# Feature sums of two layer norms folded on the vector engine, so that each takes one matmul with ones

## The chip, the cores and the metric

The kernel runs on one core of one Trainium2 chip. The metric is the device time of one execution in microseconds; it is measured several times, and the median is taken.

## What is computed

A small vision tower over 64 images. Each image becomes 37 tokens (36 patches and a class token) of 256 features. Four blocks follow, each added to the tokens after a layer norm: a selective scan, dense experts (8 routed ones, weighted by a router, and a shared one of four pieces), attention (16 heads of 16 features, causal, over the 37 tokens of an image), and a routed expert layer. The norm ahead of each block is what matters here:

```
def _layernorm(x, axis=-1, eps=1e-05):
    m = jnp.mean(x, axis=axis, keepdims=True)
    v = jnp.var(x, axis=axis, keepdims=True)
    return (x - m) / jnp.sqrt(v + eps)
...
h = h + _L0_ffn_ref(_layernorm(h, axis=-1), ...)
h = h + _L1_attn_ref(_layernorm(h, axis=-1), ...)
h = h + _L1_ffn_ref(_layernorm(h, axis=-1), ...)
```

These norms are computed in 32-bit floating point.

## The kernel before, in words

Features lie on the 128 partitions, in two halves (HALVES = 2), and tokens along the columns. The 2,368 tokens are worked on in 8 chunks of 296 columns (CH), 8 images each. The residual stream is `hF`, 128 x 2 x 2368; the normed one is `xn`, of the same form.

A sum over features is a sum over partitions and over the two halves. TensorE makes it: a 128 x 128 matrix of ones (scaled to give a mean) times the data, once for each half, both added up in one PSUM bank. One norm of a chunk goes through five helpers:

- `pe_mean` (L391): two matmuls over the halves of h, 296 columns each (L395).
- `dve_center` (L426): VectorE subtracts the mean, 592 columns at once, into xn.
- `act_square` (L410): ScalarE squares xn into `sq`.
- `pe_var` (L399): two matmuls over the halves of the squares (L403).
- `act_rstd` (L417, L420) and `dve_scale` (L433): logarithm and exponential on ScalarE for the reciprocal root, then VectorE multiplies.

Each engine has its own list of instructions, written out by hand, and the lists meet only through semaphores that count up. The norm of a chunk is woven into the work of the next one, for the two norms that matter here as follows.

**Dense experts** (570 to 756 us of the span; norm "attn"). `pe_moe`, `act_moe` and `dve_moe` (L557 to L658) go through the chunks; a chunk has 12 pieces (8 experts and 4 of the shared expert; 8 in the first two chunks). For a piece TensorE makes the up product (two matmuls, L526), ScalarE its ReLU (L609), VectorE the gate and the square (L642, L648; only L648 for the shared pieces), and TensorE two down products two steps later (L585). Chunk c - 1's mean comes on TensorE ahead of step 5 of chunk c, its variance ahead of step 8; VectorE centres it after piece 5, ScalarE squares it after piece 6; the reciprocal root and the scaling come behind the last piece, then VectorE adds the result to hF (L655). SP loads the next gates when that add is done (L663).

**Attention** (756 to 965 us; norm "moe1"). `pe_step`, `act_step` and `dve_step` go through the chunks in four steps each, p = 0 to 3, two images a step. TensorE: turn the probabilities (L1322), the values' products (L1285), the outputs' products (L1339), the score products two steps ahead (L1273), and turn the outputs (L1364). VectorE: mask and row maximum and subtraction of the next step's scores (`soften`, L1985, L1990, L1992), reciprocal and scaling of the outputs (L2015, L2023), and the spreading of values (L2004, L2007). ScalarE: copy of the turned probabilities (L1684), the exponential (L1668), copies of the turned outputs (L1697, L1698). GpSimd: spreading of the keys (L981). The output projection of chunk c - 1 is at p = 1 on TensorE (L1295), and VectorE adds it to hF (L2030); the mean is at p = 2, ahead of the router's logits (L462), the centring at the end of VectorE's p = 2, the square at the end of ScalarE's p = 2, the variance at p = 3 behind the score products; the scaling is at p = 0. Chunk 7's norm comes behind the loop in both stages.

Of the kernel before, what the change touches and what calls it, by code (L numbers as in the profile page):

```python
# [17 lines left out]
CH = IC * L  # L18
NCH = NI // IC
# [81 lines left out]
def build(nc, small, dense, patches, w_lin, a_rows, up0, dn0, w1, w2, b1, b2, gates_dram, slots,  # L101
          rows_dram, delta_dram, h_dram, gate_dram, out):
    with ExitStack() as ctx:
# [3 lines left out]
        def sem(name):  # L107
            return ctx.enter_context(nc.semaphore(name))
# [11 lines left out]
        def home(off, words, dt=F32):  # L120
            assert off + words <= REST
            return at(RING + off, words, dt)
# [9 lines left out]
        sq = home(14336, 2 * HALVES * CH).rearrange("p (j k t) -> p j k t", j=2, k=HALVES)  # L132
        rstd = home(15520, 2 * CH).rearrange("p (j t) -> p j t", j=2)
        wd = at(29952, NDENSE)
        sm = sb("sm", [P, NSMALL])
# [150 lines left out]
        embedded_ps, embedded = sem("embedded_ps"), sem("embedded")  # L286
        LN = {n: sem(f"ln_{n}") for n in ("mean", "centered", "squared", "var", "logvar", "rstd", "normed")}
        LN_FROM = {"scan": 0, "moe0": NCH, "attn": 2 * NCH, "moe1": 3 * NCH}
# [102 lines left out]
        def pe_mean(pe, s, c, bank, deep=1):  # L391
            h = hF0 if s == "scan" else hF
            pe.wait_ge(LN["centered"], LN_FROM[s] + c + 3 - deep)
            for k in range(HALVES):
                mm = nc.tensor.matmul(ps[:, bank, 0:CH], ones[:], h[:, k, ds(c * CH, CH)],  # L395
                                      start=(k == 0), stop=(k == HALVES - 1))
            mm.then_inc(LN["mean"], 1)

        def pe_var(pe, s, c, j, bank, deep=1):  # L399
            pe.wait_ge(LN["squared"], LN_FROM[s] + c + 1)  # L400
            pe.wait_ge(LN["logvar"], LN_FROM[s] + c + 3 - deep)
            for k in range(HALVES):
                mm = nc.tensor.matmul(ps[:, bank, 0:CH], ones[:], sq[:, j, k, :],  # L403
                                      start=(k == 0), stop=(k == HALVES - 1))
            mm.then_inc(LN["var"], 1)

# [16 lines left out]
        def dve_center(dve, s, c, bank):  # L423
            h = hF0 if s == "scan" else hF
            dve.wait_ge(LN["mean"], LN_FROM[s] + c + 1)
            nc.vector.tensor_tensor(xn[:, :, ds(c * CH, CH)], h[:, :, ds(c * CH, CH)],  # L426
                                    bc(ps[:, bank, 0:CH], 1, HALVES),
                                    ALU.subtract).then_inc(LN["centered"], 1)

        def dve_scale(dve, s, c, j):  # L430
# [126 lines left out]
        def pe_moe(pe, s, ln, nt, up_w, dn_w):  # L557
# [3 lines left out]
            def norm_mean(c):  # L561
                pe.wait_ge(s["h"], c + 3)
                pe.wait_ge(LN["logvar"], LN_FROM[ln] + c + 2)
                pe_mean(pe, ln, c, 0)

            def step(c, cj, on):
# [3 lines left out]
                for j in range(n + 2):  # L570
                    if on(1) and j == 5:
                        norm_mean(c - 1)
                    if on(1) and j == 8:
                        pe_var(pe, ln, c - 1, 1 - cj, 0)
# [43 lines left out]
        def dve_moe(dve, s, ln, nt):  # L618
# [3 lines left out]
            def step(c, cj, on):  # L622
                if not on(0):
                    dve_center(dve, ln, c - 1, 0)
                    dve_scale(dve, ln, c - 1, 1 - cj)
                    return
# [6 lines left out]
                for j in range(pieces(c, nt)):  # L633
# [15 lines left out]
                    if on(1) and j == 5:  # L649
                        dve_center(dve, ln, c - 1, 0)  # L650
                if on(1):
                    dve_scale(dve, ln, c - 1, 1 - cj)
                dve.wait_ge(s["down"], c + 1)
                cs = ds(c * CH, CH)
                nc.vector.tensor_tensor(hF[:, :, cs], hF[:, :, cs], ps[:, 1 + 2 * cj:3 + 2 * cj, 0:CH],  # L655
                                        ALU.add).then_inc(s["h"], 1)

            staged(dve, step, 1)  # L658
# [351 lines left out]
        def _(pe):  # L1010
# [302 lines left out]
            def pe_step(c, cj, p, more2, more1):  # L1313
# [39 lines left out]
                if p == 2 and not (isinstance(c, int) and c == 0):  # L1353
                    pe.wait_ge(attn_h, c)
                    pe_mean(pe, ln, c - 1, 7)
# [15 lines left out]
            def pe_last():  # L1371
                pe.wait_ge(attn_h, NCH - 1)
                pe.wait_ge(LN["logvar"], LN_FROM[ln] + NCH + 1)
                project(NCH - 1, 1)
                pe.wait_ge(attn_h, NCH)
                pe_mean(pe, ln, NCH - 1, 7)
                pe_logits(pe, MOE["moe1"], ln, NCH - 2, 6, w_r)
                pe_var(pe, ln, NCH - 1, 1, 7)
                pe_logits(pe, MOE["moe1"], ln, NCH - 1, 6, w_r)
# [381 lines left out]
        def _(dve):  # L1761
# [266 lines left out]
            def add_projected(c):  # L2028
                dve.wait_ge(wo_ps, c + 3)
                nc.vector.tensor_tensor(hF[:, :, ds(c * CH, CH)], hF[:, :, ds(c * CH, CH)],  # L2030
                                        ps[:, 6:8, 0:CH], ALU.add).then_inc(attn_h, 1)

            def dve_first():
                soften(0, 0, 0)
                spread_values(0, 0, 0)

            def dve_step(c, cj, p, more2, more1):
                if more1 or p < 3:
                    soften(*ahead(c, cj, p, 1))
# [10 lines left out]
            def dve_last():  # L2050
                dve_scale(dve, ln, NCH - 2, 0)
                add_projected(NCH - 1)
                dve_center(dve, ln, NCH - 1, 7)
                dve_scale(dve, ln, NCH - 1, 1)

# [200 lines left out]
```

## Time and profile before

| | us |
|---|---|
| median of 3 executions | 1154.97 (1151.09 to 1156.85) |
| the profiled execution, its own time | 1155.57 |
| its span, first to last instruction | 1153.4 |
| TensorE matmul busy | 935.1, 5925 records |
| VectorE busy | 657.2, 1129 records |
| ScalarE busy | 508.3 |
| GpSimd busy | 305.0 |

Times of the trace count from the first instruction of the span. PE is TensorE's matmuls, DVE is VectorE, ACT ScalarE, POOL GpSimd. One fp32 matmul leaves two records, whose times overlap; the chain of waits shows what it takes of the engine's time. PEclk is the granted clock of TensorE, 1.00 being 2.4 GHz and 0.50 being 1.2 GHz.

### The profile page before, as it was taken

Reading aid. Unit: us, or ns where it says so; the run is one execution under the profiler, and the core shown is the slowest. Engines: PE = TensorE matmul, PEld = TensorE weight load, DVE = VectorE, ACT = ScalarE, POOL = GpSimd, SP = SyncE. Lnnn points to the kernel's source line nnn. Section 1 sums busy time; section 2 is a strip of 40 time slices with the busy share of each in tenths; the row PEclk is TensorE's granted clock in tenths of the full one; section 3 lists DMA queues with packets and bytes.
Section 4 is the critical chain, followed back from the end, with each engine's and each line's share of the span. In section 5 each row is a group of like instructions: output and inputs, shape, how many; then the busy total and the mean of one; then the engine's idle time right before and its main releaser. Section 6 shows DMA issues by size and latency. Waiting matters only on the chain.

```text
span 1153.4 us, 17650 instructions
## 1 busy us (share of the span) xinstructions
PE 935.1 (81%) x5925; PEld 597.4 (52%) x5926; DVE 657.2 (57%) x1129; ACT 508.3 (44%) x1028; POOL 305.0 (26%) x361
## 2 busy tenths in 40 slices
PE   8996272677777777669999999989999997559996
PEld 6763230233333233235677777757767664336564
DVE  2534833588888889865454444437777673313332
ACT  1227371777777887424322222234444532223332
POOL 5913911133333430000000000035444430422222
PEclk9999656898898998989999999979999998579999
DMA  6292369422222211434521111000000000522230
GB/s 234 92 344 94 96 198 237 95 51 51 50 52 50 53 32 34 175 149 199 180 70 58 42 42 42 0 1 1 1 1 0 0 2 1 222 100 83 78 94 25
DMA packets 92705, 96.06 MB, mean 83 GB/s; under 512 B 64350, under 2 KB 78687, under 8 KB 90976
## 3 DMA queue, kind: packets, MB, share of 16 engines
q1 hardware_dynamic: 89904, 87.91, 25.1%
q0 software_dynamic: 2736, 7.30, 1.7%
q8 instruction: 39, 0.64, 0.2%
q14 instruction: 26, 0.21, 0.1%
HBM read 61.57 MB, written 34.59 MB: 83 GB/s over the span
## 4 chain that ended last, share of the span: by engine, by line
PE 64%; ACT 12%; DVE 9%; issue 6%; SPq 4%; DMA 4%; another core or an unknown queue 0%; POOL 0%; ACTq 0%; DVEq 0%; POOLq 0%
PE ps L526 8%; PE ps L585 8%; PE ps L1142 6%; ACT mem L1572 5%; PE ps L1024 4%; PE ps L1428 4%; PE ps L1444 4%; PE ps L1339 3%; PE ps L1273 3%; PE ps L395 3%; PE ps L1102 3%; PE ps L403 3%; SPq L783 2%; ACT mem L1597 2%; PE ps L1285 2%
## 5 line engine op out<-in xcount | busy, mean ns | idle before, releaser
L981 POOL TENSOR_TENSOR mem<-mem,sm 128x296 f32<-128x296 f32 x128 | 87.0, 713 | 364.3 <-ACT mem L1662 321.5
L1572 ACT ACTIVATE mem<-ps 128x512 f32<-128x512 f32 x288 | 154.0, 637 | 42.9 <-DMA factor_rows<-mem 30.3
L959 POOL TENSOR_SCALAR mem<-mem,sm 128x16 f32<-128x16 f32 x148 | 102.7, 716 | 203.5 <-PE ps L1142 203.5
L1102 PE MATMUL ps<-mem 64*128 64x128 bf16 x1140 | 92.0, 230 | 53.6 <-ACT mem L1572 44.3
L1102 PEld LDWEIGHTS ps<-mem 64*128 64x128 bf16 x1140 | 56.0, 99 | 121.6 <-ACT mem L1572 102.4
L1883 DVE TENSOR_TENSOR ps<-mem 128x512 f32<-128x512 f32 x144 | 93.5, 694 | 42.1 <-ACT mem L1597 41.6
L526 PE MATMUL ps<-mem 128*128 (+1 forms) x384 | 108.6, 413 | 0.6 <-DVE mem L499 0.6
L1597 ACT ACTIVATE mem<-ps 128x512 f32<-128x512 f32 x148 | 82.4, 609 | 54.0 <-PE ps L1109 53.8
L1142 PE MATMUL ps<-mem 128*32 128x512 f32 x592 | 87.3, 663 | 22.1 <-issue 13.6
L1109 PE MATMUL ps<-mem 64*128 64x512 bf16 x296 | 76.7, 421 | 31.5 <-DVE ps L1883 21.6
L1875 DVE TENSOR_TENSOR mem<-mem 128x1024 f32<-128x1024 f32 x72 | 87.7, 1218 | 25.0 <-ACT mem L1572 25.0
L585 PE MATMUL ps<-mem 128*128 128x296 f32 x352 | 99.7, 413 | 2.2 <-DVE mem L648 2.2
L609 ACT ACTIVATE mem<-ps 128x296 f32<-128x296 f32 x88 | 36.7, 417 | 142.0 <-PE ps L526 142.0
L1894 DVE TENSOR_TENSOR mem<-mem,ps 128x1024 f32<-128x1024 f32 x72 | 87.4, 1213 | 1.2 <-PE ps L1109 0.7
L526 PEld LDWEIGHTS ps<-mem 128*128 128x128 f32 x384 | 72.8, 190 | 23.4 <-DVE mem L499 0.9
L585 PEld LDWEIGHTS ps<-mem 128*128 128x128 f32 x352 | 66.8, 190 | 23.4 <-DVE mem L648 2.7
L648 DVE TENSOR_TENSOR mem<-mem 128x296 f32<-128x296 f32 x88 | 41.1, 467 | 41.8 <-ACT mem L609 39.6
L642 DVE TENSOR_TENSOR mem<-mem 128x296 f32<-128x296 f32 x64 | 29.9, 467 | 52.2 <-ACT mem L609 46.8
L1109 PEld LDWEIGHTS ps<-mem 64*128 64x128 bf16 x296 | 21.3, 96 | 71.3 <-DVE ps L1883 54.3
L1428 PE MATMUL ps<-mem 128*128 x104 | 51.4, 618 | 7.7 <-issue 7.1
L1024 PE MATMUL ps<-mem 128*128 128x288 f32 x192 | 50.5, 416 | 5.1 <-DMA mem<-in_patches 5.1
L433 DVE TENSOR_TENSOR mem<-mem 128x592 f32 (+1 forms) x32 | 26.1, 816 | 49.2 <-ACT mem L420 49.2
(224 smaller groups left out, 1613.0 us busy)
## 6 DMA issues: line engine op xcount, KB each, us to landing
mem<-gates SPq DMA_DIRECT2D x7, 1184.0 KB, 6.1
mem<-in_w SPq DMA_DIRECT2D x2, 4096.0 KB, 17.5
slots<-mem SPq DMA_DIRECT2D x1, 6682.0 KB, 23.8
mem<-slots SPq DMA_DIRECT2D x26, 257.0 KB, 2.7
mem<-in_patches SPq DMA_DIRECT2D x7, 864.0 KB, 4.8
mem<-factor_rows SPq DMA_DIRECT2D x296, 16.0 KB, 1.8
mem<-factor_rows SPq DMA_DIRECT2D x37, 128.0 KB, 2.3
mem<-delta_rows SPq DMA_DIRECT2D x9, 512.0 KB, 4.5
```

What stands on the lines that cost most here:

```text
L526: mm = nc.tensor.matmul(ps[:, bank, 0:CH], w[:, k, row0:row0 + P], xn[:, k, cols], start=(k == 0), stop=(k == HALVES - 1))
L585: mm = nc.tensor.matmul(ps[:, 1 + 2 * cj + m, 0:CH], dn_w[:, j - 2, m * P:(m + 1) * P], hid2[:, b, :], start=(j == 2 and n == nt), stop=(j ...
L959: nc.gpsimd.tensor_scalar(c_win4[:, t % SLOTS * 2 + r, :, w0:w0 + 8].rearrange("p j (x i) -> p j x i", i=2)[:, :, :, i], c_all[:, r * 16:r ...
L1024: mm = nc.tensor.matmul(ps[:, 2 * j + m, 0:IC * NP], wl[:, f, m * P:(m + 1) * P], xin[:, j, f, :], start=(f == 0), stop=(f == FK - 1))
L1102: mm = nc.tensor.matmul(ps[:, ring_bank(at_), e * BT:(e + 1) * BT], a_stat[64 * r:64 * r + 64, g, e, :], delta_in[b % 2][64 * r:64 * r + 6 ...
L1109: return nc.tensor.matmul(ps[:, bank, :], b_in[t % INJ][rows, m, :], dx_in[t % INJ][rows, m, :, :].rearrange("p x n -> p (x n)"), start=st ...
L1142: mm = nc.tensor.matmul(ps[32 * j:32 * j + 32, Y_BANK, :], c_win[:, win:win + 32], slot[slot_of(t)][:, quad * 512:(quad + 1) * 512], start ...
L1428: mm = nc.tensor.matmul(ps[:, 2 + j, 0:HID1], slot_xT[j][:, k, :], w1s[:, k, ds(e * HID1, HID1)], start=(k == 0), stop=(k == 1))
L1572: nc.scalar.activation(decay_slots[b % 2][:, :, 4 * k:4 * k + 4], ps[:, ring_bank(at_), :].rearrange("p (e t) -> p t e", e=4), ACT.Exp).th ...
L1597: nc.scalar.activation(slot[slot_of(t)][:, quad * 512:(quad + 1) * 512], ps[:, GROW_BANK + half, :], ACT.Copy).then_inc(copied, 1)
L1875: nc.vector.tensor_tensor(now[:, gs], now[:, gs], before[:, gs], ALU.mult).then_inc(multed, 1)
L1883: nc.vector.tensor_tensor(ps[:, GROW_BANK + half, :], now[:, hs], before[:, hs], ALU.mult).then_inc(seeded, 1)
```

## The change

For the norms "attn" and "moe1" VectorE adds up the two halves before TensorE sums over partitions. Behind each residual add it adds the two halves of h into a buffer `hsum` of 296 columns (`dve_sum`), and when the squares are there, it adds their two halves in place (`dve_fold`). `pe_mean` and `pe_var` then take one matmul each in place of two, and wait for a new semaphore, "halved", that counts two for a chunk. The buffer is a single one, so the sum waits for the mean of the chunk before. In the dense experts the fold stands behind piece 7, and the variance goes from ahead of step 8 to ahead of step 9; in the attention the fold is the first thing in VectorE's p = 3, ahead of `soften`. TensorE's waits on the residual add ahead of the mean are taken out. The change's description in words also says that attention products alternate the two images; the diff has no line on that. The norms "scan" and "moe0" stay as they are.

```
+        hsum = home(16112, CH)
...
+        HALVED = {"attn": 0, "moe1": NCH}
...
         def pe_mean(pe, s, c, bank, deep=1):
             h = hF0 if s == "scan" else hF
+            if s in HALVED:
+                pe.wait_ge(LN["halved"], 2 * (HALVED[s] + c) + 1)
             pe.wait_ge(LN["centered"], LN_FROM[s] + c + 3 - deep)
+            if s in HALVED:
+                nc.tensor.matmul(ps[:, bank, 0:CH], ones[:], hsum, start=True, stop=True).then_inc(LN["mean"], 1)
+                return
...
         def pe_var(pe, s, c, j, bank, deep=1):
-            pe.wait_ge(LN["squared"], LN_FROM[s] + c + 1)
+            if s in HALVED:
+                pe.wait_ge(LN["halved"], 2 * (HALVED[s] + c) + 2)
+            else:
+                pe.wait_ge(LN["squared"], LN_FROM[s] + c + 1)
             pe.wait_ge(LN["logvar"], LN_FROM[s] + c + 3 - deep)
+            if s in HALVED:
+                nc.tensor.matmul(ps[:, bank, 0:CH], ones[:], sq[:, j, 0, :],
+                                 start=True, stop=True).then_inc(LN["var"], 1)
+                return
...
+        def dve_sum(dve, s, c, ready, n):
+            h = hF
+            dve.wait_ge(ready, n)
+            dve.wait_ge(LN["mean"], LN_FROM[s] + c)
+            nc.vector.tensor_tensor(hsum, h[:, 0, ds(c * CH, CH)], h[:, 1, ds(c * CH, CH)],
+                                    ALU.add).then_inc(LN["halved"], 1)
+
+        def dve_fold(dve, s, c, j):
+            dve.wait_ge(LN["squared"], LN_FROM[s] + c + 1)
+            nc.vector.tensor_tensor(sq[:, j, 0, :], sq[:, j, 0, :], sq[:, j, 1, :],
+                                    ALU.add).then_inc(LN["halved"], 1)
...
             def norm_mean(c):
-                pe.wait_ge(s["h"], c + 3)
...
-                    if on(1) and j == 8:
+                    if on(1) and j == 9:
                         pe_var(pe, ln, c - 1, 1 - cj, 0)
...
             def step(c, cj, on):
                 if not on(0):
                     dve_center(dve, ln, c - 1, 0)
+                    dve_fold(dve, ln, c - 1, 1 - cj)
                     dve_scale(dve, ln, c - 1, 1 - cj)
...
                     if on(1) and j == 5:
                         dve_center(dve, ln, c - 1, 0)
+                    if on(1) and j == 7:
+                        dve_fold(dve, ln, c - 1, 1 - cj)
...
                 nc.vector.tensor_tensor(hF[:, :, cs], hF[:, :, cs], ps[:, 1 + 2 * cj:3 + 2 * cj, 0:CH],
                                         ALU.add).then_inc(s["h"], 1)
+                dve_sum(dve, ln, c, s["h"], c + 3)
...
                 if p == 2 and not (isinstance(c, int) and c == 0):
-                    pe.wait_ge(attn_h, c)
                     pe_mean(pe, ln, c - 1, 7)
...
                 project(NCH - 1, 1)
-                pe.wait_ge(attn_h, NCH)
                 pe_mean(pe, ln, NCH - 1, 7)
...
                 nc.vector.tensor_tensor(hF[:, :, ds(c * CH, CH)], hF[:, :, ds(c * CH, CH)],
                                         ps[:, 6:8, 0:CH], ALU.add).then_inc(attn_h, 1)
+                dve_sum(dve, ln, c, attn_h, c + 1)
...
             def dve_step(c, cj, p, more2, more1):
+                if p == 3 and not (isinstance(c, int) and c == 0):
+                    dve_fold(dve, ln, c - 1, 1 - cj)
                 if more1 or p < 3:
                     soften(*ahead(c, cj, p, 1))
...
                 dve_center(dve, ln, NCH - 1, 7)
+                dve_fold(dve, ln, NCH - 1, 1)
                 dve_scale(dve, ln, NCH - 1, 1)
```

## Rows read from the trace of the kernel before

**Rows 1.** Busy time by stretch: stretch, its length, engines' busy us, PEclk, DMA share, GB/s

```profile
570.00:752.00 182.00, 182.00 (x733) 138.75 (x732) 83.50 (x168) 44.40 (x103) 0.00 (x0) 1.00 0.16 47
...
766.00:778.00 12.00, 11.04 (x53) 6.29 (x50) 5.92 (x8) 2.62 (x4) 7.96 (x12) 0.50 0.01 2
778.00:960.00 182.00, 177.23 (x1546) 127.92 (x1543) 132.43 (x296) 77.23 (x171) 76.14 (x112) 1.00 0.00 1
```

**Rows 2.** Chain that ended last, dense experts: start us, us, what

```profile
608.38 1.00 PE ps L395 x4
...
634.30 1.00 PE ps L395 x4
...
641.27 1.00 PE ps L403 x4
```

**Rows 3.** Order of time, dense experts, one chunk: start us, us, what, idle before

```profile
626.50 0.77 DVE L655 TENSOR_TENSOR mem<-mem,ps 128x592 f32 x1 [0.93 <-PE ps L585]
...
627.81 0.47 DVE L642 TENSOR_TENSOR mem<-mem 128x296 f32<-128x296 f32 x1 [0.54 <-ACT mem L609]
...
638.63 0.70 ACT L410 ACTIVATE mem<-mem 128x592 f32 x1
...
641.26 0.47 DVE L648 TENSOR_TENSOR mem<-mem 128x296 f32<-128x296 f32 x1
```

**Rows 4.** Order of time, dense experts, from the second chunk to the third

```profile
599.48 0.78 DVE L433 TENSOR_TENSOR mem<-mem 128x592 f32<-128x592 f32 x1 [1.60 <-ACT mem L420]
...
600.45 0.77 DVE L655 TENSOR_TENSOR mem<-mem,ps 128x592 f32<-128x592 f32 x1 [0.20 <-PE ps L585]
...
603.24 1.16 PE L585 MATMUL ps<-mem 128*128 128x296 f32 x4
```

**Rows 5.** Order of time between the two stages, last chunk's norm

```profile
756.88 1.26 PE L395 MATMUL ps<-mem,ones 128*128 128x296 f32 x4
...
759.74 1.26 PE L403 MATMUL ps<-mem,ones 128*128 128x296 f32 x4 [0.40 <-ACT mem L410]
```

**Rows 6.** Chain that ended last, attention, one chunk

```profile
860.04 1.19 PE ps L395 x4
...
865.80 1.00 PE ps L1273 x7
866.80 1.19 PE ps L403 x4
...
878.90 2.19 PE ps L1295 x8
...
885.08 1.19 PE ps L395 x4
```

**Rows 7.** Order of time, attention, third and fourth step of a chunk

```profile
861.38 0.77 DVE L426 TENSOR_TENSOR mem<-mem,ps 128x592 f32 x1 [0.59 <-PE ps L395]
...
862.07 0.77 DVE L1985 TENSOR_TENSOR mem<-ps,sm 101x592 f32<-101x592 f32 x1
...
862.95 0.70 ACT L410 ACTIVATE mem<-mem 128x592 f32 x1
...
863.67 0.78 DVE L1992 TENSOR_TENSOR mem<-mem 101x592 f32<-101x592 f32 x1
...
865.84 0.27 DVE L2015 RECIPROCAL mem<-ps 101x18 f32<-101x18 f32 x1 [1.39 <-PE ps L1339]
866.15 0.55 DVE L2023 TENSOR_TENSOR mem<-ps,mem 101x96 f32<-101x96 f32 x3
...
868.21 0.23 ACT L1697 ACTIVATE mem<-ps 128x74 f32<-128x74 f32 x1 [3.03 <-PE ps L1364]
```

**Rows 8.** Order of time, attention: GpSimd's bursts and VectorE beside them

```profile
866.89 2.63 POOL L981 TENSOR_TENSOR mem<-mem,sm 128x296 f32<-128x296 f32 x4 [4.14 <-PE ps L1273]
...
868.95 1.20 DVE L1992 TENSOR_TENSOR mem<-mem 101x592 f32<-101x592 f32 x1
...
876.72 5.69 POOL L981 TENSOR_TENSOR mem<-mem,sm 128x296 f32<-128x296 f32 x8 [7.20 <-ACT mem L1662]
...
881.27 0.77 DVE L2030 TENSOR_TENSOR mem<-mem,ps 128x592 f32 x1 [1.74 <-PE ps L1295]
```

More of the change, by code:

```diff
@@ L286, in build @@
         embedded_ps, embedded = sem("embedded_ps"), sem("embedded")
-        LN = {n: sem(f"ln_{n}") for n in ("mean", "centered", "squared", "var", "logvar", "rstd", "normed")}
+        LN = {n: sem(f"ln_{n}") for n in ("halved", "mean", "centered", "squared", "var", "logvar", "rstd", "normed")}
+        HALVED = {"attn": 0, "moe1": NCH}
         LN_FROM = {"scan": 0, "moe0": NCH, "attn": 2 * NCH, "moe1": 3 * NCH}
```

## The prediction

> **What bounds the kernel now.** I read, in this order, the busy times by stretch, the chain of waits that ended last, and the order of time around one chunk of each stage. The two stages that the change touches are the dense experts (570 to 752 us) and the attention (about 765 to 960). In [rows 1] TensorE is busy in 182.00 of 182 us in the first, VectorE in 83.5; in the second TensorE has 177.2 of 182 us, VectorE 132.4. Both at full granted clock (1.00, the 2.4 GHz level); between them lie 12 us at 0.50, the 1.2 GHz level. So the dense stage is TensorE's alone, and the attention nearly so: what shortens TensorE's list there should shorten the stage, as long as VectorE's longer list does not come to the fore. That is the question of this case.
>
> **What is removed.** In each of 8 chunks of both stages, the sum over 256 features for the mean is two matmuls with the matrix of ones, and that for the variance two more. One of each pair goes: 2 x 2 x 8 = 32 matmuls. In the chain [rows 2] a pair is four records (each fp32 matmul is two) and takes 1.00 us of TensorE's time; one matmul is worth 0.50 us. The busy mean of a record is not used, since records overlap.
>
> **Dense stage, gain.** Seven means and seven variances lie inside the loop (that of the last chunk comes after it). TensorE has no gap, so 14 x 0.50 = 7.0 us, if no new wait arises. Three places could make one.
> - The fold (squares' halves added on VectorE) needs the squares, which ScalarE has from 638.63 + 0.70 = 639.33, and stands behind the product that ends at 641.26 + 0.47 = 641.73 [rows 3]. In the new order TensorE is 0.5 us earlier there and VectorE with it, so the fold ends near 641.7. The variance matmul, moved from before the up and down products of step 8 to step 9, comes at 641.3 - 0.5 + 2.0 = 642.8. Slack 1.0 us; the cost is 0. Without the move it would have been a stall of about 0.9 us a chunk.
> - The sum of h's halves stands after the residual add: 626.50 + 0.77 = 627.27, and the next work of VectorE starts at 627.81 [rows 3]. An add of that very shape (128x296, both operands in SBUF) takes 0.47, so it fills the gap of 0.54 and costs 0.
> - The second chunk has 8 pieces, not 12, so its variance stands last but one. Today its scaling starts at 599.48 and the residual add at 600.45, and the first down product of the next chunk at 603.24, 0.37 after its operand [rows 4]. With the variance one place later the scaling stays at 599.5 though all else is 1.0 us earlier; then the add, 0.47 for the sum and two products of 0.47: operand at about 602.5, wanted at 602.24. One loss of 0.3 us.
> Dense: -6.7.
>
> **Between the stages.** The last chunk's norm is a chain through all engines. Residual add, mean, centring, square, variance [rows 5]: twice 0.47 plus a hop between engines (0.05) enters, twice 0.50 leaves. I take 0 (bounds -0.1 and +0.3). The same chain ends the attention: 0 again.
>
> **Attention, gain of the mean.** One chunk is four steps and lasts 25.04 us, 860.04 to 885.08 [rows 6]. In the third TensorE does the mean (860.04, 1.19 us, [rows 6]) with work before and behind it; 0.5 us goes there. The centring today waits for it and starts at 861.38 [rows 7]. VectorE's list before it is now longer by the sum, added in the second step behind the residual add at 881.27 (the same place one chunk on, [rows 8]). Its price: 0.47 alone. But GpSimd is at work there until 876.72 + 5.69 = 882.41, and [rows 8] shows what that does: the subtraction of 592 columns, both operands in SBUF, takes 0.78 without GpSimd [rows 7], and 1.20 started at 868.95 while GpSimd's burst of four runs to 869.52. So the sum may take up to one more GpSimd operation, 5.69 / 8 = 0.71, on top. I take 0.7: it could start at 881.27 + 0.77 = 882.04 and would be held to 882.41. VectorE has 0.59 us of waiting before the centring [rows 7], so the centring stays near 861.5, and the square (at 862.95 today behind the output copies, 862.45 then) is not held. The Trainium skill (page "SBUF — State Buffer", section "SBUF: two separate sides") says that a VectorE instruction with two SBUF inputs and a GpSimd one that reads SBUF exclude each other, each holding the ports for its whole length. The trace agrees in size (0.42 more); by the rule read strictly the sum would take at most 1.2 us, which changes the total by nothing unless GpSimd is the one held.
>
> **Attention, gain of the variance.** Here the fold heads the fourth step on VectorE, ahead of the softmax's three operations (add of the mask, row maximum, subtraction), which today run at 862.07 right behind the centring and end at 863.67 + 0.78 = 864.45 [rows 7]. Queued behind the fold are all of them, then the scaling of the outputs, for which TensorE's transposes wait. The fold waits for ScalarE's square: 862.45 + 0.70 = 863.15. Fold 863.2 to 863.67; the three then end at 866.05. The output scaling (reciprocal at 865.84 after 1.39 us of waiting for the products, three multiplies from 866.15 to 866.70) would be due 0.5 earlier, at 865.34, and starts at 866.05: its last result comes at 866.9. TensorE's variance takes from 866.80 to 868.00 today [rows 6] and the transposes follow; then it would run from 866.3 to 866.8, and the transposes wait for the multiplies, about 0.2 us. ScalarE's copy behind them, at 868.21 today, comes at 867.45: -0.76 a chunk in place of the full -1.0. From there the chain goes through ScalarE (logarithm, exponential, the copy of the compressed rows) and shifts as a whole; VectorE waits again in each of the next two steps. Six chunks so: -4.6. The last step of the last chunk has no softmax ahead of it: -1.0. Attention: -5.6, bounds 0 (VectorE eats all) and -7.0.
>
> **The sum.** -6.7 + 0 - 5.6 + 0 = -12.3 us. The profiled execution took 1155.57 us (span 1153.4), 0.6 above the median of 1154.97 shown. From the median: **1142.7 us**. Stages after the attention are untouched and start earlier. Loads of gates on SP's queue wait for the residual adds as before, and no queue is passed. The added waits are on the semaphore of the halves; TensorE's older waits on the residual add go, which the new ones imply.
>
> **Rivals.**
> 1. **VectorE eats the attention's gain.** For it: the fold's wait of about 1.1 us behind the centring, with 73% of VectorE busy. Against: 1.39 us of waiting at the reciprocal [rows 7], so the overrun is only 0.2. Then only the dense stage pays: 1155.0 - 6.7 = 1148.3.
> 2. **VectorE becomes the path (the slower side).** In the fourth step its list ends later by 863.67 - 861.57 = 2.1 us than centring alone would let it, and by 0.7 in the second. If no waiting absorbed that, 7 x 2.8 = 19.6 us enter, the attention's gain is nil, and the dense 6.7 leave: 1168. It decides where the fourth step's softmax ends over 2.7 us later than today: 1.39 of waiting [rows 7] and 1.3 from the last multiply (866.15 + 0.55) to the transposes (868.00). Mine ends 1.6 later, so the square would have to come over 1.1 us later than I have it.
> 3. **The clock.** After the short waits at the stages' border the clock stands at 0.50 for 12 us [rows 1], 11 of them busy. TensorE has less to do there now. If that low stretch became twice as long, half of 11 us is added: 1142.7 + 5.5 = 1148.2; if it went, 5.5 less. The Trainium skill (page "TensorE: Matmul & The Clock Gate", section "What's actually happening") has the half rate as the state that too little activity brings back. That the clock holds 1.00 through waits of 0.7 us in each chunk speaks against more of it.
> 4. **Not as said.** The words also speak of attention products that alternate the two images; no line of the diff touches them. Nor is there a gain left: score products of 64 and 37 output rows already run two at a time, seven records in 1.00 us where eight full-width ones take 2.19 [rows 6]. If the norms had no effect either, 1155.
>
> **How the numbers follow.** Forecast 0.72; rival 1 0.12; rival 2 0.05; the clock 0.07; rival 4 0.04. A measurement of this kernel tells from no change about 0.5%, 5.8 us, so the border is 1149.2. The three runs spread by 5.8 us. Rivals 1 and 3 stand just below the border, and I give 0.06 of their 0.19 to "same", with rival 4 0.10; faster 0.85; slower 0.05. The range: low, all 28 matmuls at full worth (-14.0) and 1.5 for scatter, 1139.5; high, rivals 1 and 3 at 1148.3 with a little of the scatter, 1148.8.
>
> **What would show it.** Dense chunk from mean to mean 24.9 us, not 25.9 (608.38 to 634.30, [rows 2]), TensorE still without a gap, the pairs in the chain two records in 0.5 us. In the attention the reciprocal of the fourth step follows the subtraction with no waiting, the transposes wait about 0.2 us for the multiplies, and the chunk lasts 24.25 us, not 25.0. The sum beside GpSimd takes about 0.7, elsewhere 0.47. Wrong if TensorE waits in the dense stage for the fold, or if the attention's chunk stays at 25 us: then VectorE's list has taken over.

## The result and the profile after

Ten runs of each kernel: 1149.56 us median (1145.89 to 1151.82) after, 1155.91 us (1151.09 to 1158.05) before; ratio 0.9945, 95% interval 0.9928 to 0.9963. So the change makes the kernel 6.4 us faster where 12.3 were forecast. The profiled execution took 1147.44 us, its span 1145.6, 7.8 less than that of before. The sign was right; the size was not, and 1149.56 lies above the range of 1139.5 to 1148.8.

The page of the kernel after (its span, its first part's row of busy times, the granted clock in 40 slices):

```profile
span 1145.6 us, 17578 instructions
...
PE 926.5 (81%) x5861; PEld 587.7 (51%) x5862; DVE 666.4 (58%) x1161; ACT 509.1 (44%) x1028; POOL 305.4 (27%) x361
...
PEclk9998656798899988989999999979999997579999
```

TensorE has 64 records less (32 matmuls), VectorE 32 instructions more and 9.2 us more of busy time. Busy time by stretch, kernel after, the columns as in [rows 1]:

```profile
570.00:752.00 182.00, 181.05 (x724) 137.15 (x724) 92.18 (x188) 45.73 (x106) 0.00 (x0) 1.00 0.16 50
752.00:766.00 14.00, 10.19 (x33) 4.61 (x32) 5.22 (x10) 5.59 (x9) 7.61 (x12) 0.71 0.00 0
766.00:778.00 12.00, 12.00 (x69) 8.56 (x66) 6.89 (x15) 3.94 (x8) 3.29 (x5) 0.63 0.01 2
778.00:960.00 182.00, 173.85 (x1525) 123.50 (x1523) 134.83 (x309) 78.78 (x174) 76.24 (x112) 0.98 0.00 1
```

The kernel before, in the second of these stretches:

```profile
752.00:766.00 14.00, 11.26 (x42) 6.97 (x42) 3.75 (x7) 6.85 (x12) 2.93 (x5) 1.00 0.00 0
```

The dense experts are still TensorE's alone. Two things are new. Between the stages the clock is low already ahead of 766 us (0.71, not 1.00). And the last row has 0.98, not 1.00, so the clock is low somewhere ahead of 960 us. The chain that ended last, kernel after, dense experts (L554 up, L612 down products, L399 mean, L413 variance):

```profile
604.27 1.22 PE ps L612 x4
...
609.48 0.50 PE ps L399 x2
...
634.40 0.50 PE ps L399 x2
...
642.87 0.50 PE ps L413 x2
```

Against [rows 2], a mean is two records and 0.50 us, and from one mean to the next it is 24.92 us, not 25.92. The chunk behind the second starts with two down products in 1.22 us instead of 1.00: the one loss that was forecast there, 0.22 for 0.3. The same chain in the attention:

```profile
829.69 0.70 PE ps L399 x2
...
835.97 0.70 PE ps L413 x2
...
853.78 0.69 PE ps L399 x2
```

The chunk is 24.09 us long, against 25.04 in [rows 6]. That is 0.95 less, where 0.76 was forecast. Order of time in the third and fourth step, kernel after (L440 centring, L424 square, L455 the fold, L2014 and L2021 the first and last operation of the softmax, L2044 and L2052 reciprocal and multiplies, L1726 the output copy):

```profile
831.06 0.76 DVE L440 TENSOR_TENSOR mem<-mem,ps 128x592 f32 x1
...
832.11 0.70 ACT L424 ACTIVATE mem<-mem 128x592 f32 x1
...
832.84 0.47 DVE L455 TENSOR_TENSOR mem<-mem 128x296 f32<-128x296 f32 x1 [1.02 <-ACT mem L424]
...
833.23 0.77 DVE L2014 TENSOR_TENSOR mem<-ps,sm 101x592 f32<-101x592 f32 x1
...
834.83 0.77 DVE L2021 TENSOR_TENSOR mem<-mem 101x592 f32<-101x592 f32 x1
...
835.52 0.26 DVE L2044 RECIPROCAL mem<-ps 101x18 f32<-101x18 f32 x1
...
835.82 0.55 DVE L2052 TENSOR_TENSOR mem<-ps,mem 101x96 f32<-101x96 f32 x3
...
836.88 0.23 ACT L1726 ACTIVATE mem<-ps 128x74 f32<-128x74 f32 x1 [0.54 <-PE ps L1394]
```

What stood in [rows 7] as 1.39 us of waiting at the reciprocal is gone, as forecast: VectorE waits 1.02 ahead of the fold instead. But the output copy comes 7.19 us after the mean's start in the chain (836.88 - 829.69), against 8.17 before (868.21 - 860.04 of [rows 6, 7]): 0.98 less, nearly the whole 1.0. The fold costs nothing, and the transposes do not wait for the multiplies. Two things in the working were off. I had laid recorded durations end to end, and the next operation of VectorE starts ahead of the recorded end of the one before (833.23 is 0.39 after 832.84, 835.52 is 0.69 after 834.83), about 0.08 sooner each. And I had let the new variance end at 866.8, where its start at 866.30 and 1.19 - 0.50 us of length give 866.99. By that sum alone it ends behind the last multiply (866.9), and nothing of the 1.0 is lost.

The sum, one step earlier (L2059 residual add, L449 the sum, POOL GpSimd's key spreading), kernel after:

```profile
847.85 3.26 POOL L1012 TENSOR_TENSOR mem<-mem,sm 128x296 f32<-128x296 f32 x5
...
849.96 0.77 DVE L2059 TENSOR_TENSOR mem<-mem,ps 128x592 f32 x1 [1.74 <-PE ps L1326]
...
850.88 0.56 DVE L449 TENSOR_TENSOR mem<-mem 128x296 f32 x1
851.36 0.76 DVE L2014 TENSOR_TENSOR mem<-ps,sm 101x592 f32<-101x592 f32 x1
```

GpSimd is at work until 847.85 + 3.26 = 851.11. The sum beside it takes 0.56 (0.47 to 0.80 over its 16 instances), and the softmax behind it starts 1.40 after the residual add, not 0.69 as in the trace before: 0.71 of delay for the 0.7 forecast.

So far there is more gain than forecast. Where it went is behind the last chunk. Order of time in the last chunk, first of the kernel before (L1339 output products, L1295 the last projection), then of the kernel after (L1370 output products, L413 the variance, L1326 the last projection):

```profile
961.19 1.25 PE L1339 MATMUL ps<-mem 111*64 111x51 f32 x24 [1.28 <-ACT mem L1684]
...
964.70 2.23 PE L1295 MATMUL ps<-mem 128*128 128x296 f32 x8 [0.89 <-ACT mem L417]
```

```profile
951.05 1.26 PE L1370 MATMUL ps<-mem 111*64 111x51 f32 x24 [1.74 <-ACT mem L1713]
952.23 1.26 PE L413 MATMUL ps<-mem,ones 128*128 128x296 f32 x2
...
954.74 4.29 PE L1326 MATMUL ps<-mem 128*128 128x296 f32 x8 [0.89 <-ACT mem L431]
```

The last projection takes 4.29 us, not 2.23, and TensorE's wait ahead of the output products is 1.74 us, not 1.28. In both kernels these products start 9.7 us after the projection before them (951.05 - 941.37, and 961.19 - 951.48): they wait for ScalarE's copy of the probabilities (L1713, before L1684), and that copy did not come sooner. The half microsecond that the mean no longer takes is only more waiting here. Busy time of 952 to 960 us, first of the kernel before, then of the kernel after:

```profile
952.00:960.00 8.00, 7.92 (x59) 5.35 (x58) 5.64 (x13) 2.36 (x7) 0.00 (x0) 1.00 0.00 0
```

```profile
952.00:960.00 8.00, 6.14 (x19) 3.39 (x16) 2.50 (x7) 1.20 (x4) 0.00 (x0) 0.57 0.00 0
```

The clock stands at 0.57 on the mean, that is at 1.2 GHz for most of it, where before it stayed at 2.4 GHz to about 974 us.

### The profile page after: what moved, and what is told of

The parts are those of the page before. It is cut to its first block, busy times and chain, and to the rows that moved or that the text cites. A ratio compares the mean times of both kernels' runs of the same rounds, so it can differ in the third digit from the quotient of the medians.

```text
span 1145.6 us, 17578 instructions
## 1 busy us (share of the span) xinstructions
PE 926.5 (81%) x5861; PEld 587.7 (51%) x5862; DVE 666.4 (58%) x1161; ACT 509.1 (44%) x1028; POOL 305.4 (27%) x361
## 4 chain that ended last, share of the span: by engine, by line
PE 63%; ACT 12%; DVE 10%; issue 6%; SPq 4%; DMA 3%; another core or an unknown queue 0%; POOL 0%; ACTq 0%; DVEq 0%; POOLq 0%
PE ps L554 8%; PE ps L612 8%; PE ps L1173 6%; ACT mem L1601 5%; PE ps L1055 4%; PE ps L1457 4%; PE ps L1473 4%; PE ps L1370 3%; PE ps L1304 3%; PE ps L1133 3%; SPq L814 2%; ACT mem L1626 2%; PE ps L1326 2%; PE ps L1140 2%; DVE mem L1904 2%
## 5 line engine op out<-in xcount | busy, mean ns | idle before, releaser
L1133 PE MATMUL ps<-mem 64*128 64x128 bf16 x1140 | 92.0, 230 | 53.5 <-ACT mem L1601 44.2
L554 PE MATMUL ps<-mem 128*128 (+1 forms) x384 | 108.6, 413 | 0.6 <-DVE mem L527 0.6
L612 PE MATMUL ps<-mem 128*128 128x296 f32 x352 | 99.9, 413 | 1.8 <-DVE mem L676 1.8
L554 PEld LDWEIGHTS ps<-mem 128*128 128x128 f32 x384 | 72.8, 190 | 23.4 <-DVE mem L527 0.9
L612 PEld LDWEIGHTS ps<-mem 128*128 128x128 f32 x352 | 66.5, 190 | 23.5 <-DVE mem L676 3.2
L1031 POOL DMA_INDIRECT out_h<-mem,slot_token x26 | 25.6, 985 | 103.5 <-DVE mem L2174 103.5
```

The source lines that it names most:

```text
L554: mm = nc.tensor.matmul(ps[:, bank, 0:CH], w[:, k, row0:row0 + P], xn[:, k, cols], start=(k == 0), stop=(k == HALVES - 1))
L612: mm = nc.tensor.matmul(ps[:, 1 + 2 * cj + m, 0:CH], dn_w[:, j - 2, m * P:(m + 1) * P], hid2[:, b, :], start=(j == 2 and n == nt), stop=(j ...
L1133: mm = nc.tensor.matmul(ps[:, ring_bank(at_), e * BT:(e + 1) * BT], a_stat[64 * r:64 * r + 64, g, e, :], delta_in[b % 2][64 * r:64 * r + 6 ...
```

## The experiments

Sixteen more executions were profiled. Every trace was cut at five marks: the start of the first down product of the dense experts, the end of the last one, the start of the first projection of the attention, that of the last but one, and the turning of the router's logits. "Border" is the stretch from the last down product to the first projection, and "last" the one from the last but one projection to the turned logits. All in us:

| kernel and trace | dense start | dense | border | six chunks | last | rest |
|---|---|---|---|---|---|---|
| before | 569.3 | 186.6 | 48.7 | 146.9 | 26.0 | 175.9 |
| before_again | 569.5 | 186.6 | 48.6 | 146.9 | 26.0 | 175.2 |
| before_third | 571.9 | 186.6 | 43.4 | 146.8 | 24.9 | 172.5 |
| before_fourth | 571.9 | 186.6 | 43.4 | 146.9 | 24.9 | 172.6 |
| sem_shift | 569.6 | 186.6 | 43.4 | 146.9 | 24.9 | 172.5 |
| before_fill_entry | 573.4 | 186.6 | 44.2 | 146.8 | 24.9 | 174.8 |
| dense_only | 571.0 | 181.8 | 47.7 | 146.6 | 24.9 | 174.8 |
| attn_only | 571.4 | 188.3 | 43.4 | 141.4 | 28.3 | 175.1 |
| after | 571.0 | 180.1 | 48.9 | 141.4 | 28.2 | 176.0 |
| after_again | 572.9 | 180.1 | 48.8 | 141.4 | 28.3 | 174.8 |
| after_third | 573.9 | 180.1 | 48.7 | 141.3 | 28.3 | 175.8 |
| after_fourth | 573.5 | 180.1 | 45.9 | 141.3 | 28.3 | 175.8 |
| sum_later | 574.4 | 180.1 | 48.9 | 141.4 | 25.0 | 175.8 |
| sum_later_again | 572.8 | 180.1 | 48.9 | 141.3 | 25.0 | 175.0 |
| fill_end | 574.6 | 181.8 | 47.6 | 141.4 | 25.5 | 177.1 |
| fill_entry | 573.4 | 181.8 | 43.6 | 141.4 | 28.3 | 175.3 |
| fill_both_late | 571.6 | 180.1 | 48.1 | 141.4 | 26.1 | 174.7 |
| fill_both_late_again | 571.5 | 180.1 | 43.6 | 141.3 | 26.1 | 176.3 |

These sixteen came in four sets, each on a chip of its own: (1) dense_only, attn_only, after_again, before_again; (2) fill_end, fill_entry, sum_later, fill_both_late; (3) before_third, before_fourth, sem_shift, before_fill_entry; (4) after_third, after_fourth, sum_later_again, fill_both_late_again. A ratio is to runs of the kernel before on the same chip; it is not exactly the quotient of the two medians. Only times of one set can be compared.

**One norm alone** (dense_only, attn_only). For the first, the attention's edits are undone; for the second, those in the dense experts:

```
-        HALVED = {"attn": 0, "moe1": NCH}
+        HALVED = {"attn": 0}              # dense_only
+        HALVED = {"moe1": 0}              # attn_only
```

> The halves are added on VectorE only for the norm that follows the dense experts; the attention's norm is as before. Theory 1 (each stage pays by itself; what is short of the forecast was lost in the attention, at its last chunk, where TensorE's clock fell early): 6.5 us less than the kernel before, ratio 0.9944. From the first up product of the dense experts (569.25 in the trace before) to the last down product (755.89) 6.5 us less. Theory 2 (half of the forecast is lost ahead of the dense stage, where the profile of the changed kernel stood 1.7 us later, by something that the change does to the whole program): 4 to 5 us less, with the dense stage starting 1 to 2 us late again.

> The halves are added on VectorE only for the attention's norm; the dense experts are as before. Theory 1: chunks 2 to 6 of the attention 24.1 us each, not 25.04 (5 x 0.95 = 4.7 us), little from the first, and 1 to 3 us given back behind the last chunk, where the clock falls to 0.50 about 20 us earlier than before: between 0 and 4 us less, ratio about 0.998. Theory 2 (nothing lost in the attention, all upstream): 5.5 us less, and no low clock before the routing.

dense_only: 1150.19 us beside 1156.22, ratio 0.9952 (0.9936 to 0.9968). attn_only: 1150.17, 0.9966 (0.9946 to 0.9986). The dense stage does pay by itself. Its length has two values 1.7 us apart, by whether the clock is low for some 3 us near its start (granted clock of 572 to 576 us: 0.57 in dense_only and attn_only, 1.00 in the kernel before): 180.1 and 181.8 with the change, 186.6 and 188.3 (attn_only) without. Like with like, that is 6.5 us less; dense_only's own trace, with the clock low there, has 4.8 less than the kernel before. Both ratios together would be 0.9918; the whole change on this chip has 0.9940 (0.9916 to 0.9964), so the times alone do not show that anything was lost in between. The traces do: attn_only has six chunks 5.5 us shorter, and "last" 28.3, longer than before by 2.3.

**The same kernels again** (after_again, before_again).

> The changed kernel once more, for a second profile beside the first. Theory 1: the time again about 1149.5, the start of the dense stage anywhere within 2 us of that of the kernel before, and the clock's early fall in the last chunk of the attention there again. Theory 2: the dense stage again starts about 1.7 us late.

> The kernel before once more, one look. Both theories need the scatter of the stages that are the same in both kernels: theory 1 has the start of the dense stage scatter by about 2 us between two profiles of one kernel, theory 2 has it back at 569.3 within 0.5. The clock should fall behind the attention at about 973 us again, not before.

after_again: 1148.3 us, ratio 0.9940 (0.9916 to 0.9964). Its lengths of the dense stage, the border, the six chunks and "last" repeat to 0.1 us, and the low clock in the last chunk is there again. before_again took 1155.05 us, and its clock fell behind the attention at 974 us, as expected. But the dense stage started at 572.9 in the one and at 569.5 in the other, in the same instructions up to there: both theories stayed in play.

**Scatter or a cost upstream** (before_third, before_fourth, sem_shift). The last of them is

```
-        LN = {n: sem(f"ln_{n}") for n in ("mean", ...
+        LN = {n: sem(f"ln_{n}") for n in ("halved", "mean", ...
```

> The kernel before again, one look. In two traces of it the dense stage starts at 569.3 and 569.5 us, in eight of kernels with the change or parts of it at 571.0 to 574.6, though all are the same instructions up to there. Theory A (scatter of the first 110 us, from loads, GpSimd beside VectorE and the clock at 90 us): this one may lie anywhere from 569 to 574. Theory B (something of the change delays the first stages by about 2.5 us): within 0.5 of 569.4.

> The same as the run above, for a fourth start of the dense stage in the kernel before. Theory A: at least one of the two beyond 570.5. Theory B: both at 569.4 within 0.5. In both theories the dense stage takes 186.6 us, or 188.3 with the clock low at its start.

> The kernel before with one semaphore more, that nothing uses, in the place where the change adds its own; each later semaphore so gets the next number. Theory A: ratio 1.000 to the kernel before within its interval. Theory B, if it is the numbers: 2 to 3 us slower, dense stage from about 572.

sem_shift: ratio 1.0001 (0.9971 to 1.0031). The dense stage started at 571.9 twice in the kernel before, and at 573.4 in before_fill_entry, which is the kernel before up to there. So it scatters by 4 us without the change, most of it already there at 115 us, and the numbering costs nothing within the interval. That the change adds nothing on top of the scatter is not shown. Something else came out of these traces: the border takes 43.4 us, not 48.7, in three of them. Busy time of 768 to 776 us, first of the kernel before in its first trace, then of before_third:

```profile
768.00:776.00 8.00, 7.18 (x26) 4.39 (x26) 5.66 (x8) 1.37 (x2) 5.96 (x9) 0.50 0.01 2
```

```profile
768.00:776.00 8.00, 6.20 (x51) 3.87 (x52) 5.07 (x8) 1.69 (x3) 8.00 (x13) 1.00 0.01 2
```

The same eight records of score products, first in the one trace, then in the other:

```profile
765.79 2.07 PE L1273 MATMUL ps<-mem 128*64 128x296 f32 x8 [1.58 <-issue]
```

```profile
768.47 1.20 PE L1273 MATMUL ps<-mem 128*64 128x296 f32 x8 [1.58 <-issue]
```

The wait ahead is the same 1.58 us in both, and the clock falls behind it in one only. In the kernel before, the low clock of [rows 1] is a matter of the execution, and is worth 5.3 us.

With the changed dense norm it is another fall. TensorE's first three waits behind the last down product, kernel after:

```profile
752.72 0.74 PE L399 MATMUL ps<-mem,ones 128*128 128x296 f32 x2 [0.65 <-issue]
...
755.55 0.77 PE L413 MATMUL ps<-mem,ones 128*128 128x296 f32 x2 [0.90 <-DVE mem L455]
...
758.26 2.34 PE L1272 MATMUL ps<-mem 128*128 128x296 f32 x4 [0.75 <-ACT mem L1691]
```

Before, the mean had no wait there and the variance one of 0.40 ([rows 5]); the sum and the fold make the new ones. The clock falls at 758 us, 7 us behind the last down product, where before it fell 10 us behind it, at 766. The waits of 0.65 and 0.90 and a fall 6 to 7 us behind the last down product are in all eight traces with the changed dense norm and no fill there, and in none of the other ten. On the chip of after_again and dense_only, which have it, before_again has the late fall and attn_only none; so this is no matter of the chip.

**Filling TensorE's idle time** (fill_end, fill_entry, before_fill_entry). Matmuls into banks that nobody reads, at places where TensorE waits; the first fill of fill_entry also waits for the residual add. Both edits are shown in part: fill_entry adds 6 matmuls in four places, fill_end 15 in five.

```
+        def pe_fill(n, bank):
+            for _ in range(n):
+                nc.tensor.matmul(ps[:, bank, 0:CH], ones[:], hF[:, 0, 0:CH], start=True, stop=True)
...
                 compress(0)
+                pe.wait_ge(MOE["moe0"]["h"], NCH + 1)
+                pe_fill(1, 1)             # fill_entry
                 last_mean(NCH - 1)
...
+                elif isinstance(c, int) and c == NCH - 1:
+                    pe.wait_ge(masked, 4 * NCH + 1)
+                    pe_fill(5, 0)         # fill_end
```

> The changed kernel with 15 matmuls more in TensorE's idle time in the last chunk of the attention and behind it (5 ahead of the wait for the last output products, 1, 3, 3 and 3 around the last norm; their results are read by nobody). Theory 1 (in the last chunk VectorE, longer by the sum, holds TensorE, whose clock then falls at 952 us and makes the last projection 4.3 us long, not 2.2): the clock stays at 1.00 there, and from the projection at 941 us to the router's turned logits 2 to 3 us less than the 28.2 of the changed kernel, total about 1147. Rival (the low clock there costs nothing, since the chain goes through VectorE and ScalarE): no change, or 1 to 3 us more for the added matmuls.

> The changed kernel with 6 matmuls more in TensorE's idle time between the dense experts and the attention (1 ahead of the last mean, 2 ahead of its variance, 1 and 2 ahead of the first scores; read by nobody). Theory 1: the low clock of 757 to 775 us goes, as it was absent in the trace with the attention's norm changed alone (there the way from the last down product to the first projection took 43.4 us, not 48.7 to 48.9): up to 5 us less, total about 1144.5. Rival (the fall is set by more than these gaps, or cannot be bought with so few): within 1 us of the changed kernel, or slower by the 3 us that the matmuls take.

> The kernel before with the 6 matmuls more in TensorE's idle time between the dense experts and the attention, as in the run that filled the entry of the changed kernel. If the low clock there is a matter of these gaps: it goes here too, the way from the last down product to the first projection takes about 43.5 us, not 48.7, and the kernel is 4 to 5 us faster, without any of the change. If not: within 1 us of the kernel before.

fill_end: 1144.79 us beside 1155.99, ratio 0.9906 (0.9872 to 0.9939); "last" 25.5, not 28.3. The rival falls: the low clock there costs about 3 us of that stretch, though 15 matmuls were added. fill_entry: 1142.76, 0.9897 (0.9862 to 0.9933), border 43.6, "last" 28.3 as without; with the wait ahead of the mean at 0.16 us and that ahead of the variance gone, the early fall is gone too. The change as made was not timed on this chip, so what each fill is worth in total time is not shown by these two runs. before_fill_entry: 1149.45 beside 1152.55, 0.9981 (0.9956 to 1.0005): border 44.2, but on that chip the kernel before had 43.4 by itself in both traces, so it shows nothing of the fill.

**The sum behind the softmax** (sum_later and again).

```
                                         ps[:, 6:8, 0:CH], ALU.add).then_inc(attn_h, 1)
-                dve_sum(dve, ln, c, attn_h, c + 1)
...
                 if more1 or p < 3:
                     soften(*ahead(c, cj, p, 1))
+                if p == 2 and not (isinstance(c, int) and c == 0):
+                    dve_sum(dve, ln, c - 1, attn_h, c)
...
                 add_projected(NCH - 1)
+                dve_sum(dve, ln, NCH - 1, attn_h, NCH)
```

> The changed kernel with the sum of h's halves in the attention moved from ahead of the third step's softmax to behind it. Theory 1: in the last chunk and the first the softmax starts 0.5 to 0.8 us earlier, and TensorE waits that much less; the fall of the clock at 952 us may go with it: 0.5 to 3 us less than the changed kernel. Middle chunks stay at 24.1 us. Rival (the sum ahead of the softmax is hidden in the last chunk as well): no change; if the mean matmul now waits for the sum, middle chunks 0.2 to 0.5 us longer, 1 to 3 us more in total.

> The changed kernel with the sum behind the softmax, second trace. Theory: no fall in the last chunk again, from the last but one projection to the turned logits 25.0 us, not 28.2; median 2 to 3 us under that of the changed kernel on this chip. Rival (chance): the fall is there, no difference.

sum_later: 1144.41 us, ratio 0.9909 (0.9874 to 0.9943); again, on another chip: 1148.34 beside 1155.72, 0.9932 (0.9911 to 0.9953). Both traces have "last" at 25.0, 3.3 us less than the change as made, and the middle chunks are the same. The fall is gone, but not because TensorE is busier. Busy time of the 10 us from the last but one projection on, ahead of the fall, first of the kernel after, then of sum_later_again:

```profile
941.37:951.37 10.00, 8.26 (x64) 5.76 (x64) 7.09 (x17) 3.88 (x10) 0.00 (x0) 1.00 0.01 2
```

```profile
943.14:953.14 10.00, 8.18 (x61) 5.60 (x61) 7.00 (x17) 3.76 (x10) 0.00 (x0) 1.00 0.01 2
```

What differs is how the waiting is spread: in place of one wait of 1.74 us there are two, ahead of the mean and ahead of the output products (sum_later_again):

```profile
948.94 0.77 PE L399 MATMUL ps<-mem,ones 128*128 128x296 f32 x2 [0.55 <-DVE mem L449]
...
952.99 1.25 PE L1370 MATMUL ps<-mem 111*64 111x51 f32 x24 [1.28 <-ACT mem L1713]
```

The last projection takes 2.25 us again, in the chain of sum_later:

```profile
958.07 2.25 PE ps L1326 x8
```

**Two more looks at the change** (after_third, after_fourth), beside the version with the sum moved and both fills (fill_both_late and again). The first of these two ran beside fill_end and sum_later, the second beside after_third and sum_later_again:

> The changed kernel, third trace, timed beside the two versions below on one chip. Theory (clock): dense stage 180.1 or 181.8 us; last chunk and what follows to the turned logits 28.2 us, with the clock at 0.50 from about 952 us; border either 48.8 (clock low) or about 43.5, more often 48.8. Rival (the fall in the last chunk is chance too): it is absent in one of the two more traces of this kernel.

> The changed kernel, fourth trace. Theory (clock): as the run above. If the border is low in both, it has been low in four of four, against two of five without the change.

> All three together: sum behind the softmax, idle time filled at the attention's entry and end. Theory 1: effects add up, about 1142. Rival: within 2 us of the best of the three alone, or no better than the changed kernel.

> Sum behind the softmax and idle time filled at both places, second trace. If the fill at the border makes the fall rarer: border near 43.5 us, median 1 to 4 us under the version with the sum moved alone. Rival: no difference between the two, the fill buys nothing that lasts.

after_third: 1149.1 us beside 1155.72, ratio 0.9935 (0.9921 to 0.9949). after_fourth, one execution, took 1146.66. Both traces have "last" at 28.3, so the low clock is there in six of six traces with the attention's sum ahead of the softmax and no fill at the end, and in none of the twelve others. fill_both_late: 1142.24, 0.9891 (0.9853 to 0.9928), and again 1142.07, 0.9881 (0.9865 to 0.9896), on one chip with after_third: 7 us better than the change and 6 better than sum_later_again there, with intervals apart, and faster than both kernels. Its two traces have borders of 48.1 and 43.6: the early fall is absent in all three traces with the changed dense norm and the fill, but in the first of these two the clock falls 12 us behind the last down product, so the fill does not exclude a low clock. The end fill costs 1.1 us where the moved sum had already removed the fall (26.1 for 25.0).

On that chip sum_later_again and after_third are not told apart by time (0.9932 and 0.9935), though the traces differ by 3.3 us in "last"; the runs of the former spread over 8 us. Expected were 2 to 3 us. So what the moved sum alone is worth is shown in the traces and not in the medians.

## Why the prediction was wrong

Term by term, forecast and measured in the first pair of traces:

- **Dense experts**: -6.7 forecast, -6.5 measured (186.6 to 180.1). Right, with its steps: no wait for the fold, one loss behind the second chunk.
- **The attention's chunks**: -4.6 forecast for six, -5.5 measured (146.9 to 141.4). The queue behind the fold was right, its price 0.2 a chunk too high: the slip in the variance's end (866.8 for 866.99) and durations laid end to end, as said above.
- **"The last step of the last chunk has no softmax ahead of it: -1.0", and the norm behind the loop: 0.** This is the step that failed: +2.2 (26.0 to 28.2), and against the traces in which the clock stays up until later (24.9) it is 3.4 more. Two parts can be told apart. The -1.0 does not come even at 2.4 GHz: in the two traces with the sum moved "last" is 25.0, against 24.9. TensorE has no score products left in the last chunk, and the way from the residual add to the centring on VectorE, and from there through ScalarE's square and copy, holds its output products where they were (5.0 us from add to centring with the sum ahead, 4.5 before); what TensorE saves it waits. And the longer wait goes with a term that the sum did not have: the clock falls to 1.2 GHz as the variance inside the last chunk starts (952 us). The last projection takes 2.1 us more, that variance again the 0.5 that it had saved; with the products beside them 3.3 us in all (28.3 against 25.0).
- **Between the stages: 0.** +0.2 with the clock low in both traces. But it is low in all eight traces with the changed dense norm and no fill there (in after_fourth the border is 45.9, between the two values), and in two of six traces without the changed dense norm and without a fill (before and before_again; not before_third, before_fourth, sem_shift, attn_only). Where it is low only after the change, 5.3 us of the gain are lost. Rival 3 had the place, and its price of the 12 us at 0.50 was near (5.5, where the border differs by 5.3), at a chance of 0.07. What it named, a low stretch twice as long, did not come: the stretch went from some 14 us to 17 and the border grew by 0.2. I had taken the low stretch as a property of the kernel that could only get longer or shorter, not as one that four of those six traces do not have.

The pair sums to -6.5 + 0.2 - 5.5 + 2.2 = -9.6; 1.7 of later start and 0.1 behind leave the 7.8 of the spans. The medians are 6.4 apart. Executions of the kernel before that are without the low border would account for some of the rest, but how many there are is open: three of the four such traces come from one chip, where that kernel was also the fastest (1152.55, against 1155.7 to 1156.2 on the others), and none of the ten runs beside the first pair took less than 1151.09, where before_third and before_fourth took 1148.3. Rivals 1 and 2 fell: VectorE ate nothing of the middle chunks. Of rival 4, the diff was all there was.

Not settled: why these waits and no others bring the clock down. In the last chunk the fall goes with the one wait of 1.74 us; it is absent where that wait is 1.28 (the kernel before, the sum moved) or filled. At the border the early fall comes behind waits of which none is over 0.90 us, so the longest wait is not the whole of it, and the late one comes or not behind the same 1.58 us. The Trainium skill (page "TensorE: Matmul & The Clock Gate", section "What's actually happening") has the half rate follow from too little activity. fill_end and fill_entry agree; the busy time of the 10 us ahead (8.26 us with the fall, 8.18 without) does not show it.

## What to carry to other kernels

Where one engine has no gap, a removed instruction pays its whole distance in the chain, here 0.50 us a matmul, and work given to another engine was free where that engine still waited somewhere behind it. Price the ends of a stage by themselves: in the last round the usual cover is missing, a removed matmul became a longer wait, and the clock that fell behind it took back what more than three chunks gave (3.3 us against 0.95 a chunk). Before a stretch at the low clock is read as part of a kernel, look at a second and third execution of it.

## What was not expected of the hardware

- One kernel, the same instructions: the border takes 43.4 or 48.7 us, by whether the granted clock stays at 2.4 GHz or is at 1.2 GHz for some 14 us. The dense stage has two lengths 1.7 us apart in the same way, but never in two traces of one kernel, only in kernels whose instructions there are the same.
- One wait of 1.74 us in place of 1.28 at the end of the attention goes with a clock that falls in six traces of six, against none of the twelve without it; what follows takes 3.3 us more.
- Added matmuls whose results nobody reads made the kernel faster: 21 of them at both ends of the attention took the version with the sum moved from 1148.34 to 1142.07 us on one chip. 15 of them at its end took "last" from 28.3 to 25.5 us in the change as made.
- VectorE's operations follow each other about 0.08 us ahead of the recorded end, so a chain of them is shorter than the sum of its durations.
